# A cross-network and MLP tower on one core: x0's rows by two transposes, row numbers straight from the ids, the filter in one go, GpSimd ends x2

## What is computed

```python
e = jnp.stack([tbl_f[ids[:, f]] for f in range(39)], axis=1)      # 512 x 39 x 16
x0 = xk = e
for W in (f0, f1, f2):
    z = jnp.einsum('bfd,bgd->bfgd', x0, xk).reshape(b, f * g, d)
    xk = jnp.einsum('bpd,pm->bmd', z, W);  outs.append(xk)        # 128 features
z = jnp.sum(jnp.concatenate(outs, axis=1), axis=-1)
h = jnp.concatenate([z, dense_ctx], axis=1)
h = jnp.maximum(h @ W_top1 + b_top1, 0.0);  h = jnp.maximum(h @ W_top2 + b_top2, 0.0)
y = h @ W_top3
```

## Time and profile before

| what | us |
|---|---|
| median of 3 runs (lowest, highest) | 704.47 (702.53, 704.82) |
| profiled execution, whole time | 706.52 |
| its span, first to last instruction | 704.7 |
| TensorE busy | 654.0 (93%) |
| VectorE, ScalarE, GpSimd busy | 600.2, 382.1, 508.1 |
| first layer 2 matmul of tile 0 | at 48.74 |
| last tile's end of layer 2, about | 682 |

### The profile page before, as it was taken

The page is one execution under the profiler, slowest core; times in us unless marked ns, Lnnn a source line. Parts: engine busy times, 40 slices in busy tenths (PEclk is TensorE's granted clock), DMA queues, the critical chain, the costliest instruction groups (busy, mean ns, idle before and its releaser), DMA issues.

```text
span 704.7 us, 11586 instructions
## 1 busy us (share of the span) xinstructions
PE 654.0 (93%) x2992; PEld 512.8 (73%) x2992; DVE 600.2 (85%) x2013; ACT 382.1 (54%) x1162; POOL 508.1 (72%) x466
## 2 busy tenths in 40 slices
PE   0279979999999999999999999999999999999997
PEld 0256757776767788787867778788777878788877
DVE  4279898999999999989679999999779898988670
ACT  1146554665656474746446565646457474655431
POOL 6747977797889888786769889786758878463320
PEclk9979989999999999999999999999999999999999
DMA  7527530303031211304030220404030130300000
GB/s 145 139 70 227 145 80 6 109 9 108 9 102 16 76 41 38 79 9 107 5 108 9 54 63 8 108 6 111 5 105 11 38 79 4 106 1 1 1 1 2
DMA packets 70517, 41.28 MB, mean 59 GB/s; under 512 B 47553, under 2 KB 55297, under 8 KB 70322
## 3 DMA queue, kind: packets, MB, share of 16 engines
q1 hardware_dynamic: 58530, 35.67, 18.8%
q10 hardware_dynamic: 6672, 3.58, 2.2%
q0 software_dynamic: 5248, 1.29, 1.8%
HBM read 38.55 MB, written 1.94 MB: 57 GB/s over the span
## 4 chain that ended last, share of the span: by engine, by line
PE 73%; DVE 12%; issue 5%; POOL 4%; ACT 3%; DMA 1%; another core or an unknown queue 1%; SPq 0%; DVEq 0%; POOLq 0%; ACTq 0%
PE y L842 18%; PE y L844 16%; PE y L843 16%; DVE scaled L733 9%; PE late L860 4%; PE side L849 4%; PE acc L813 3%; PE acc L819 3%; PE acc L814 3%; POOL emb_quads L452 2%; ACT scaled L562 2%; PE y L860 1%; PE late L871 1%; PE late L903 1%; DVE z L703 1%
## 5 line engine op out<-in xcount | busy, mean ns | idle before, releaser
L733 DVE SCALAR_TENSOR_TENSOR scaled<-y,x_rows,scaled 128x128 f32<-128x128 f32 x1728 | 471.5, 341 | 57.0 <-ACT scaled L562 32.5
L562 ACT ACTIVATE scaled<-y,x_rows 128x128 f32<-128x128 f32 x768 | 218.7, 367 | 228.9 <-PE y L844 210.9
L842 PE MATMUL y<-w_hi,x_parts 128*128 128x512 f32 (+1 forms) x640 | 284.1, 444 | 11.3 <-DVE scaled L733 7.2
L844 PE MATMUL y<-w_hi,x_parts 128*128 128x512 f32 (+1 forms) x640 | 250.4, 391 | 0.0
L843 PE MATMUL y<-w_lo,x_parts 128*128 128x512 f32 (+1 forms) x640 | 250.3, 391 | 0.0
L463 POOL TENSOR_TENSOR z_parts<-z,z_parts 117x512 fp32r<-117x512 f32 (+1 forms) x107 | 138.7, 1296 | 44.7 <-ACT z_parts L512 39.3
L842 PEld LDWEIGHTS y<-w_hi,x_parts 128*128 128x128 f32 x640 | 121.3, 190 | 62.9 <-DVE scaled L733 30.9
L452 POOL DMA_INDIRECT emb_quads<-in_small_tables_dram,quad_rows x144 | 139.2, 966 | 25.1 <-issue 11.8
L844 PEld LDWEIGHTS y<-w_hi,x_parts 128*128 128x128 f32 x640 | 121.1, 189 | 26.4
L843 PEld LDWEIGHTS y<-w_lo,x_parts 128*128 128x128 f32 x640 | 121.9, 190 | 18.4
L471 POOL TENSOR_TENSOR sum<-scaled 128x512 f32<-128x512 f32 x64 | 83.2, 1300 | 69.5 <-DVE x_sb L741 59.8
(11 more groups left out here) (85 smaller groups left out, 370.9 us busy)
## 6 DMA issues: line engine op xcount, KB each, us to landing
z<-x_turned SPq DMA_DIRECT2D x320, 78.0 KB
x_three<-x_turned SPq DMA_DIRECT2D x48, 78.0 KB
x_turned<-emb_quads SPq DMA_DIRECT2D x156, 8.0 KB
w_sb<-in_w_dram SPq DMA_DIRECT2D x1, 2496.0 KB, 9.4
emb_quads<-in_small_tables_dram,quad_rows POOLq DMA_INDIRECT x144
s_sb<-in_w_dram ACTq DMA_DIRECT2D x28, 80.0 KB
x_turned<-emb_singles SPq DMA_DIRECT2D x95, 2.0 KB
wt_sb<-in_W_top_dram SPq DMA_DIRECT2D x1, 768.0 KB
```

Source lines behind the costliest of these rows:

```text
L562: done = act.activation(scaled[:, k % 2, BY_ACT.index(j), i * M:(i + 1) * M], y2[n % RING][:, i * M:(i + 1) * M], ACT.Copy, scale=x0_rows[ ...
L733: dve.scalar_tensor_tensor(part, y2[n % RING][:, i * M:(i + 1) * M], x0_f, part, ALU.mult, ALU.add).then_inc(terms_in, 1)
L842: pe.matmul(dst, x1_hi[:, t % 2, cols], hi, start=True, stop=False)
L844: pe.matmul(dst, x1_lo[:, t % 2, cols], hi, start=False, stop=True).then_inc(y_ready, 1)
```

## The change

x0's rows: three of a tile's four 128 column blocks of x0 are read by three further DMAs of SP into `x0_stack` (39 rows each, 117 partitions), and one transpose turns them at once, a second one the fourth block. Row numbers: the array `ids_four` and its eight DMAs go; DVE adds to `ids_sb`, tile by tile, 4 times 14 small additions for the first group and 4 times 14 for the rest, all ahead of tile 0, in place of 14 ahead of it and 14 in tile 1. The filter comes in four pieces, all issued by ACT at the start, and all four low parts are made by DVE before the first product. POOL ends x2 and DVE's `x2_of` goes. The places of the chunks and of x1 move. Tile 0's transposes stand behind its fifth contraction and ACT copies them behind all high parts. Five gathers of group 1 are spread over tiles 0 and 1.

```diff
-CHUNKS_AT = (0, 4, 7, 11, 14, 18, 21)
+CHUNKS_AT = (0, 4, 8, 12, 16, 20, 24)
...
-X1_AT = 31
+X1_AT = 34
...
-    cuts = (0, 0, 0, 0, len(SINGLES)) if g == 1 else (0, 0, 0, 3, len(SINGLES))
+    cuts = (0, 0, 0, 3, len(SINGLES))
...
+            def three_blocks(u):
+                if u >= 2:
+                    sp.wait_ge(rows_t, u - 1)
+                for k in range(3):
+                    sp.dma_start(x0_stack[F * k:F * k + F, u % 2, :], x0_dram[u, 0:F, P * k:P * k + P]).then_inc(stack_in[u % 2], 16)
...
                     turned_rows(sp, u, c)
+                    if c == 2:
+                        three_blocks(u)
...
+                pool.wait_ge(two_in, k + 1)
+                if k >= 2:
+                    pool.wait_ge(s_ready, k - 1)
+                pool.tensor_tensor(x2_sb[:, k % 2, :], sum2[:, 0:M], sum2[:, M:2 * M], ALU.add).then_inc(x2_in, 1)
...
-            second_filter_low(W1_EARLY + 1)
...
-            load_filter(act, 0)
+            for j in range(W1_PIECES):
+                load_filter(act, j)
...
-            rows(0)
             for c in range(C0):
                 high_part(0, c)
...
+            rows(0)
...
-            dve.wait_ge(four_ids_in, 64)
-            quad_numbers(slice(0, TPG)).then_inc(quads_first, 1)
+            dve.wait_ge(ids_in, 16)
+            for q in range(TPG):
+                quad_numbers(slice(0, 1), q).then_inc(quads_first, 1)
...
+            dve.wait_ge(rest_ids_in, 16)
+            for q in range(TPG):
+                quad_numbers(slice(1, GROUPS), q).then_inc(quads_rest, 1)
...
-            for i in range(W1_EARLY):
+            for i in range(W1_PIECES):
                 second_filter_low(i)
...
-                    if s % BANKS == X2_AT and n > BANKS:
-                        x2_of(n // BANKS - 1)
-                    if t == 1 and s == REST_AT:
-                        dve.wait_ge(rest_ids_in, 80)
-                        quad_numbers(slice(TPG, TILES)).then_inc(quads_rest, 1)
...
-                for k in range(NBLK):
-                    mm = pe.transpose(side[:, k * F:(k + 1) * F], x0_three[0:F, u % 2, k * P:(k + 1) * P], ident[0:F, 0:F])
-                mm.then_inc(rows_t, 1)
+                pe.wait_ge(stack_in[u % 2], 48 * (u // 2 + 1))
+                pe.transpose(side[:, 0:3 * F], x0_stack[0:3 * F, u % 2, :], ident[0:3 * F, 0:3 * F])
+                pe.transpose(side[:, 3 * F:NBLK * F], x0_three[0:F, u % 2, 3 * P:NBLK * P], ident[0:F, 0:F]).then_inc(rows_t, 1)
```

More of the change, by code:

```diff
@@ L95 @@
 Y_AT = 149
[L99 to L102 removed]
+W1_PIECES = 4
 def runs(fields):
@@ L289, in cross_network @@
         weights_in = sem("weights_in")
-        w1_in = [sem(f"w1_in_{h}") for h in range(2)]
+        w1_in = [sem(f"w1_in_{j}") for j in range(W1_PIECES)]
         top_in = sem("top_in")
@@ L307, in cross_network @@
         three_up = sem("three_up")
+        stack_in = [sem(f"stack_in_{i}") for i in range(2)]
         a_in = [sem(f"a_in_{i}") for i in range(C0)]
@@ L350, in turned_rows, with load_filter @@
                 queue.dma_start(z[F * r:F * r + F, c, :], x0_dram[u, shift:shift + F, :]).then_inc(a_in[c], 16)
-        def load_filter(queue, h):
-            for j in range(4):
-                first = HALVES[h] + j
-                n = (HALVES[h + 1] - first + 3) // 4
-                for a in range(4):
-                    r = SPLIT * (HALVES[h] // 4) + (a - j) % 4
-                    queue.dma_start(w1_raw[32 * a:32 * a + 32, first:HALVES[h + 1]:4, :],
-                                    w1[32 * j:32 * j + 32, r:r + SPLIT * (n - 1) + 1:SPLIT, :]).then_inc(w1_in[h], 16)
+        def load_filter(queue, j):
+            for a in range(4):
+                r, n = (a - j) % 4, (F - j + 3) // 4
+                queue.dma_start(w1_raw[32 * a:32 * a + 32, j:F:4, :],
+                                w1[32 * j:32 * j + 32, r:SPLIT * (n - 1) + r + 1:SPLIT, :]).then_inc(w1_in[j], 16)
         def store_singles(queue, u, copies):
@@ L612, in _ @@
                     store_quad(act, 0, i, (1,))
-            load_filter(act, 1)
-            act.wait_ge(w1_in[0], 256)
-            for i in range(W1_EARLY):
-                high_filter(i)
+            for j in range(W1_PIECES):
+                act.wait_ge(w1_in[j], 64)
+                copy(w1_hi[:, j:F:4, :], w1_raw[:, j:F:4, :]).then_inc(w1_hi_in, 1)
             three(0)
-            rows(0)
             for c in range(C0):
                 high_part(0, c)
-                if c == 1:
-                    act.wait_ge(w1_in[1], 256)
-                if c in (1, 2):
-                    high_filter(W1_EARLY + c - 1)
+            rows(0)
             x1_high(0)
```

77 lines of the change are left out of this document (25 added, 52 removed).

## The result

The changed kernel takes 712.32 us (median; 709.41 to 713.71), the kernel before 704.35 beside it: ratio 1.0129, 95% interval 1.0107 to 1.0151. It is 8.0 us slower where the forecast was no change (705.0). The time lies within the range given; that nothing would change was wrong.

A forecast was written before the change was run, and what follows sets the result against it. It took PE to bound most tiles, with gains possible at the start, tiles 0 and 1 and DVE's lateness. Terms +17.1 - 1.6 - 4.4 - 6.1 + 1.6 - 6.2 = +0.4 on 704.5 gave 705.0 us, range 697 to 713.

The forecast's parts named there:

- step 6: Start: rows behind the high parts, filter loaded earlier and its subtraction off POOL, -6.2 us, bounds 0 to -8.
- rival F: Start: gains nothing, since the filter's transfers or the additions delay the gathers, 711 us; chance 0.05.
- step 1: Transposes in tiles 1 to 14: PE waits longer for ACT's copy of side, 1.22 us a tile, +17.1.
- Step 2: Transposes of each tile: two in place of four save 0.1 us in each of 16 tiles, -1.6.
- Step 3: Later tiles' first banks: DVE without the end of x2 is less late for PE, -4.4 us.
- step 4: Tile 1: its row number additions go to the start, so it resembles tile 2, -6.1 us.
- step 5: Tile 0: +2.5 us for PE's waits on POOL's low parts, -0.9 for DVE's relief, together +1.6.
- Rival D: Transposes in the tiles: the clock falls at the new waits, slower, 717 us (709 to 728); chance 0.12.
- C: Transposes: the added wait isn't there, so the kernel is faster, 688 us (685 to 692); chance 0.08.
- E: Tiles with twelve gathers: POOL becomes the bound, low parts 0.3 to 0.5 us late, 710 us; chance 0.12.

The follow-up runs named there:

- b_rows_late: The kernel before with tile 0's transposes behind the fifth contraction and the copy of the rows behind all high parts: 707.11 us, ratio 1.0008.
- b_new_places: The kernel before with only the chunk places and x1 place of the changed kernel: 721.28 us, ratio 1.0268.
- a_old_no_stack: The changed kernel with the old chunk and x1 places and without the stack, four transposes for every tile: 706.28 us, ratio 0.9987.
- b_x2_pool: The kernel before with only the end of x2 moved to GpSimd: 704.63 us, ratio 0.999.
- b_small_adds: The kernel before with the changed kernel's row numbers, 112 small additions ahead of tile 0 and none in tile 1: 709.78 us, ratio 1.0037.
- a_old_x2_dve: The changed kernel with the old chunk and x1 places and x2 ended on VectorE again: 709.43 us, ratio 1.0054.
- a_rows_29: The changed kernel with the transposes and the copy of their result two slots later (29 and 30 for 27 and 28): 697.64 us.
- b_again: The kernel before, unchanged, profiled in another execution: 707.68 us (one run).
- a_again: The changed kernel, unchanged, profiled in another execution: 724.49 us.
- a_third: The changed kernel, unchanged, timed again against the kernel before in one submission: 723.54 us, ratio 1.0233.
- b_spread_numbers: The kernel before with tile 1's 14 row number additions one at a time at even slots 0 to 26, not all at slot 6: 705.81 us, ratio 1.0029.

## Why the prediction was wrong

**The step that failed is step 6, the start (-6.2), and under it the base.** It took the 48.7 us of one execution for what the kernel needs and counted ScalarE's 5.7 us wait and the slow z transfers as things that the change removes. The runs showed the start to have a short and a long form (and 45.4 and 45.7 us between them in the last submission); moving the rows as the change does left it at 48.2 (b_rows_late). In the short form the start of before reaches layer 2 at 44.22 (b_new_places; the kernel before itself was not profiled with a short start) and the changed one at 43.5 to 44.3 (four kernels, three of them in the same submission): the gain is nothing. In the long form it is 48.2 to 49.0 against 53.9 to 57.1: a loss of 5 to 9 us, because the second 56 additions stretch from 5.9 to up to 25 us and VectorE's low parts of both filters stand behind them. The prediction had warned that the start loses if the cover of the additions is gone, and then closed its bounds at 0. What it feared was late four-field gathers; what came late were those low parts. Its rival F, that the start gains nothing, 711, had a chance of 0.05 and is what happened. The profile of before was of the long form and that of after of the short one, so that the table above shows a gain of 4.6 us that the change did not bring.

b_new_places is the clean partner of after, since both have the short start and the new places. Their spans differ by 8.9 us (719.3 and 710.4): start -0.1, tile 0 +3.0 (38.8 to 41.8), tile 1 -5.1 (42.9 to 37.8), tiles 2 to 15 -6.8 (567.9 to 561.1), behind them 0. With the 18.5 that the places cost in b_new_places, the change makes 18.5 - 8.9 = +9.6 against the 702.8 of that submission. Against the 704.35 beside it, after is only 8.0 slower: before was 1.5 us faster in the former submission than in the latter, and no trace shows why. A sum with 0 in place of -6.2 would have said +6.6, 711; the other steps are off by another 3 us together, +1.4 in step 1, -0.8 in steps 2 and 3, +1.0 in step 4 and +1.4 in step 5.

By its steps:
- Step 1, +17.1: right in mechanism and size (16.0 and 18.5 in whole times, 1.19 a tile in the traces, of 15.6 us in tiles 1 to 15 6.5 for the high part and the rest for the contraction, 0.46 and 0.65 a tile where 0.52 and 0.70 were expected).
- Step 2, -1.6: wrong in sign, +0.07 a tile, about +1. The cost bound of 0.1 that the text names was the nearer one, and a_old_no_stack shows the same from the other side (0.9 less in 14 tiles).
- Step 3, -4.4: right in sign and size, -4.0 in the kernel before; with the new places -6.8 together with step 2. The size is in part luck. The 5.1 us of recorded idle time that it is made from do not stand at the tiles' first banks: in the trace of before 3.9 stand at slots 12 and 38 and 1.2 ahead of the transposes, and 2.7 of the 3.9 are still there in b_x2_pool. Almost half of the gain, 1.9 us, came in the seven tiles in which PE shows no idle time and from which the step expected nothing.
- Step 4, -6.1: 5.1 in the short form (42.9 to 37.8), 5.0 in b_small_adds (43.0 to 38.0). It was mis-sized by 1 us. The time does go, but the additions that replace it can cost more in the start.
- Step 5, +1.6: +3.0. The relief of 0.9 wasn't there (b_new_places waits only 0.40 for VectorE in tile 0), and PE's waits for GpSimd's low parts are 3.0 in place of 2.5. They are these four in after; b_new_places has none. Below them are those of a_old_x2_dve, which has the further gathers but x2 on VectorE:

```profile
59.55 0.50 PE L796 MATMUL acc<-z_parts,w_hi 117*128 117x512 f32 x1 [1.55 <-POOL z_parts L453]
65.65 0.50 PE L796 MATMUL acc<-z_parts,w_hi 117*128 117x512 f32 x1 [0.43 <-POOL z_parts L453]
69.33 0.50 PE L796 MATMUL acc<-z_parts,w_hi 117*128 117x512 f32 x1 [0.61 <-POOL z_parts L453]
80.39 0.50 PE L796 MATMUL acc<-z_parts,w_hi 78*128 78x512 f32 x1 [0.43 <-POOL z_parts L453]
```

```profile
73.39 0.50 PE L802 MATMUL acc<-z_parts,w_hi 117*128 117x512 f32 x1 [1.27 <-POOL z_parts L454]
79.50 0.50 PE L802 MATMUL acc<-z_parts,w_hi 117*128 117x512 f32 x1 [0.43 <-POOL z_parts L454]
83.18 0.50 PE L802 MATMUL acc<-z_parts,w_hi 117*128 117x512 f32 x1 [0.61 <-POOL z_parts L454]
```

  With x2 off GpSimd 2.3 of the 3.0 us stay, and with x2 on it but without the further gathers (b_x2_pool) the waits are 1.3. So the gathers bring the larger part, which the prediction left without a price; no run moved them alone.
- Rival D did not happen: the granted clock is 1.00 from tile 0 to tile 15, with waits of 1.14 to 1.37 us by the records in 14 tiles. (It fell in tile 4 of a_rows_29, and not in tile 8, behind waits of 1.56.) Neither did C, nor E as it was put: x2 takes 0.46 us on GpSimd and the low parts stay in time behind tile 1.

The end of x2 on GpSimd, all 63 of them (shortest, median, longest ns):

```profile
L474 POOL TENSOR_TENSOR x_sb<-sum x63: 452/458/466, 56.6 to 681.4; 128x128 f32<-128x128 f32 x63
```

The straight line of the prediction gave 0.46, and one on VectorE without GpSimd in its way took 0.27. So the rule of the Trainium skill ("GPSIMD Engine Reference", section "4.1 Engine selection", about twice as slow for two inputs) holds here at 1.7 times, and moving the work was right all the same behind tile 1, since VectorE was the late engine, its mean beside GpSimd was 0.58 and not 0.27, and GpSimd had slack.

**Behind tile 15** the changed kernel took 25.5 us, before 22.6. First a stretch of after, in which the granted clock was 0.50 (1.2 of 2.4 GHz); then, in another execution of the same kernel (a_third), all that is behind tile 15:

```profile
690.00:695.00 5.00, 4.47 (x21) 4.36 (x21) 0.00 (x0) 0.75 (x2) 0.00 (x0) 0.50 0.00 0
```

```profile
697.12:719.70 22.58, 18.04 (x134) 15.35 (x133) 3.69 (x12) 3.50 (x11) 0.25 (x1) 1.00 0.00 1
```

With 6.8 us at 0.50 (689.2 to 696.0) it takes 25.5, at 1.00 throughout it takes 22.6. Before has had 22.6, and 24.2 in b_again, and b_new_places has 25.5: all three values come in kernels with and without the change, and 22.6 and 25.5 in the same kernel. It belongs to the execution, not to the change; PE's list ahead of it is the same.

**Left open:** what makes the start long in one submission and short in another. The chip alone doesn't decide it: the first two submissions ran on the same one, eleven minutes apart, the first with short starts and the second with long ones. Each kernel was profiled once in a submission, so how much the starts differ within one is not known. Instructions stand in "issue" until about 36 us from the kernel's beginning, on VectorE among small instructions, on SyncE among its z transfers (0.61 us each in the earlier trace rows, 0.41 in the short form), and nothing that the profile shows ends it. The load of the DMA engines doesn't set the two apart: it is over 90% until 20 us in after and in a_again alike, and the stops of a_again begin at 14.5.

## What to carry to other kernels

A place in an engine's list is worth what stands ahead of it between a producer and the copy that frees a PSUM bank: work out that chain for each slot before you spread work "evenly". One profiled execution is no base for a start-up that isn't bound by an engine: profile the kernel before twice, and where the executions differ, set the bounds of that step by both. Many tiny instructions ahead of a chain that others wait for are a risk of their own, even where they fit the idle time of one trace. A mean duration can hide two kinds of instruction: look at the shortest and the longest, and at what the other engines do when the long ones end.

## What the runs showed of the hardware

- 56 additions of 32 partitions by 3 numbers took 5.9 us in one piece (0.11 each) in after, and 25.1 us with stops of up to 4.6 us in a_again, the same kernel; 23 to 25 in the other long starts of the changed kernel.
- The long ones among VectorE's two-input additions all ended just behind a two-input instruction of GpSimd: 23 of the 64 of x2 in before took 0.37 to 1.96 us in place of 0.28 and ended about 0.15 us behind one; six of 14 small ones in b_spread_numbers took 0.90 to 1.66 in place of 0.16 to 0.28 and ended within 0.1 us behind one. Beside a gather of GpSimd an addition kept its short time (the one at 93.36 above, 0.16).
- One transpose of 117 rows and one of 39 took 0.43 us to the next bank, four of 39 rows 0.36 to 0.37: fewer and larger transposes were not cheaper.
- A stretch with PE at 38.53 of 38.53 us busy became 0.3 us shorter when another engine was relieved.
